# Layer 2's linear attention: the output projection in three products of rounded parts, squares summed on ScalarE, shared buffers

## The chip, the cores and the metric

The kernel runs on one core of a Trainium2 chip. The metric is the device time of one execution in microseconds; the time before is the median of three runs. A core has five engines that run their own queues of instructions in order and wait for one another by semaphores: TensorE (matrix products, "PE"; its weight loads are "PEld"), VectorE ("DVE"), ScalarE ("ACT"), GpSimd ("POOL") and SyncE ("SP"), which issues DMA transfers. Products go into PSUM, everything else lies in SBUF, 128 partitions each.

## What is computed

The reference is a model of four layers over 4 x 512 tokens of 256 channels in fp32; each layer adds an attention part and a feed-forward part to its input. The change is in the attention part of layer 2, a linear attention with 16 heads of 64 key, 64 slot and 128 value channels:

```python
q, k, v = heads(x @ Wq), heads(x @ Wk), heads(x @ Wv)
s = clip(heads(x @ Ws), -32, 32)
# per head, over time t, with p, g from the running log-sum-exp of s:
hk = hk * g_t + k_t[..., None] * p_t          # then ok_t = q_t . hk
pv = softmax(ok)
hv = hv * g_t[..., None] + p_t[..., None] * v_t   # then ov_t = pv_t . hv
g = x @ Wg
o = o * rsqrt(mean(o * o) + EPS) * g_norm_weight
o = o * (g * sigmoid(g))
y = o.reshape(b, t, VALUE_DIM) @ Wo
```

## The kernel before

The layers run one after the other, in blocks that each end at a barrier. The block of the change is `layer2_abc` (L987). Its work is cut into 32 units: 8 pairs of heads times 4 sequences of 512 tokens; `k` is a unit's place in a round of 8, `u` its number. Each engine has a function `unit` that is called 32 times, and its text is the order of the work: nothing is reordered by a scheduler. The projections of unit u + 1 are computed inside unit u, and the output of unit u - 1 is finished there.

TensorE in a unit (L1283 on): the scores of keys and queries (`scores`), the sums of each chunk of 128 tokens (`chunk_sums`), the projections s, k and q of the next unit, the logits (`ok`), the turn of the last unit's output (`turn_out`), v0, the turn of the logits, v1, the **output projection** of the last unit (`emit`, L1209), g0, the turn of the softmax weights, g1, `weights`, the turns of k and e, and `ov`, the output proper. The input projections are products of rounded parts: `split_matmul` (L108) multiplies hi by hi, hi by lo and lo by hi, where hi is the value rounded to a shorter format (fp32r) and lo what is left. The output projection (L1215) is a plain fp32 product of `w_o` and `oT`, which the trace shows as two records each.

Between a unit's output and its projection lies a chain over four engines. `pov`, in the PSUM tensor `pde`, holds the output. ScalarE squares it into `sq`, which is the buffer `on` (L1376). VectorE sums the squares of each head and chunk and scales the sum (`mean_square`, L1460 and 1461). GpSimd raises it to the power -1/2 (`rstd`, L1112) and multiplies the gate with it (`gr`, L1116). VectorE multiplies output and gate (`gated`, L1466), TensorE turns the product into `pde` (L1206), ScalarE multiplies with the norm's weight (`oT`, L1356), and TensorE projects. VectorE adds the result to `x` (L1472).

The head-pair weights are loaded by SyncE into `w_raw`, two slots, and split into `w_hi` and `w_lo` by ScalarE (L1326) and GpSimd (L1098) once for four units; the first slot is split by ScalarE and VectorE at the end of the block before (L401, L393). The weights of the output projection went unsplit into `w_o` with the same call of `load`.

Of the kernel before, what the change touches and what calls it, by code (L numbers as in the profile page):

```python
# [952 lines left out]
class AbcWeights:  # L953


    WQ, WC = 3 * DC * P, 3 * DC * P + 2 * DC * 2 * P

    def __init__(self, st, dram, raw):
        self.dram, self.PV = dram, 2 * P
        self.raw, self.parts = raw, st.sb_parts("w", [P, 2, self.WC])  # L960
        self.o = st.sb("w_o", [P, 2, 2, D])
        self.arrived, self.hi_ready, self.split = [st.sem("w0_in"), st.sem("w1_in")], st.sem("w_hi"), st.sem("w_split")
# [4 lines left out]
    def vg(self, t, slot):  # L967
        return t[:, slot, self.WQ:self.WC].rearrange("p (k c n) -> p k c n", k=2, c=DC)

    def load(self, sp, slot, hp):  # L970
        for k, n in enumerate(("Ws", "Wq", "Wk")):
            sp.dma_start(self.qks(self.raw, slot)[:, k, :, :],
                         in_chunks(self.dram["L2_attn_" + n])[:, :, bass.ds(hp * P, P)]
                         ).then_inc(self.arrived[slot], 16)
        for k, n in enumerate(("Wv", "Wg")):
            sp.dma_start(self.vg(self.raw, slot)[:, k, :, :],
                         in_chunks(self.dram["L2_attn_" + n])[:, :, bass.ds(hp * self.PV, self.PV)]
                         ).then_inc(self.arrived[slot], 16)
        sp.dma_start(self.o[:, slot, :, :], in_chunks(self.dram["L2_attn_Wo"])[:, bass.ds(hp * 2, 2), :]
                     ).then_inc(self.arrived[slot], 16)  # L980
# [6 lines left out]
def layer2_abc(nc, st, core, dram, a, w, aT, w2):  # L987
# [22 lines left out]
    w_raw, w_in_parts, w_o, w_qks, w_vg, load = w.raw, w.parts, w.o, w.qks, w.vg, w.load  # L1010
    gnorm = st.sb("gnorm", [P, 1])
    qT, kT, eT = (st.sb(n, [P, 2, T]) for n in ("qT", "kT", "eT"))
    rT, lgT = st.sb("rT", [P, 2, T]), st.sb("lgT", [P, T])
    k_tok, e_tok = (st.sb(n, [P, 2, NCH, P]) for n in ("k_tok", "e_tok"))
    v, gate = (st.sb(n, [P, 2, NCH, PV]) for n in ("v", "gate"))
    th = st.sb("th", [P, NCH, PV])
    sm, am = st.sb("sm", [P, 2, NCH, P]), st.sb("am", [P, 2, NCH, P])
    hk, hv = st.sb("hk", [P, 3, DK]), st.sb("hv", [P, 3, DV])
    lg, ex, wt = (st.sb(n, [P, NCH, P]) for n in ("lg", "ex", "wt"))
    wT = st.sb("wT", [P, T])  # L1020
    mx, den = st.sb("mx", [P, 8]), st.sb("den", [P, 8])
    on, gr = (st.sb(n, [P, 2, NCH, DV]) for n in ("on", "gr"))
    sq = on
    ms, rstd = st.sb("ms", [P, 8]), st.sb("rstd", [P, 8])
    oT = st.sb("oT", [P, 2, T])
# [9 lines left out]
             "gr_ready on_ready o_turned oT_ready y_ready y_added").split()  # L1035
# [28 lines left out]
    heads8 = lambda a: a.rearrange("t c (h m) -> t (c h) m", h=2)  # L1064

# [12 lines left out]
    with nc.Block() as block:  # L1078
# [15 lines left out]
        def _(pool):  # L1094
# [6 lines left out]
            def unit(u, k, first, last):  # L1101
# [3 lines left out]
                if u and split_in(0, (u - 1) % PER) and not ((u - 1) % PER == 5 and last_round(u - 1)):  # L1105
# [5 lines left out]
                pool.wait_ge(s["ms_step"], 2 * (u + 1))  # L1111
                pool.tensor_tensor(rstd[:], ms[:], core.consts[:, C_HALF:C_HALF + 8], ALU.pow  # L1112
# [3 lines left out]
                pool.tensor_tensor(gr[:].rearrange("t h c v -> t c h v"),  # L1116
                                   gate[:, k % 2].rearrange("t c (h v) -> t c h v", h=2),
# [7 lines left out]
        def _(pe):  # L1125
# [83 lines left out]
            def emit(u, k):  # L1209
                slot = (k // B) % 2  # L1210
                pe.wait_ge(s["oT_ready"], u + 1)
                for t in range(NCH):
                    for h in range(2):
                        cols = oT[:, h, :].rearrange("d (g q p) -> d g p q", q=P, p=2)[:, t // 2, t % 2, :]
                        ins = pe.matmul(pyy[:, t, :], cols, w_o[:, slot, h, :], start=(h == 0), stop=(h == 1))  # L1215
                ins.then_inc(s["y_ready"], 1)
# [103 lines left out]
        def _(act):  # L1320
# [22 lines left out]
            def project_g(u, k, half):  # L1343

                act.wait_ge(s["g_ready"], 2 * u + half + 1)
                act.activation(th[:, 2 * half:2 * half + 2], bank(f"g{half}")[:].rearrange("t (c v) -> t c v", v=PV),  # L1346
                               ACT.Tanh, scale=0.5).then_inc(s["tanh_ready"], 1)
# [6 lines left out]
            def emit(u):  # L1354
                act.wait_ge(s["o_turned"], u + 1)
                act.activation(oT[:], pde[:], ACT.Copy, scale=gnorm[:, 0:1]).then_inc(s["oT_ready"], 1)  # L1356

            def unit(u, k, first, last):
# [17 lines left out]
                act.activation(sq[:], pov, ACT.Square).then_inc(s["sq_ready"], 1)  # L1376
# [20 lines left out]
        def _(dve):  # L1397
# [22 lines left out]
            def project_g(u, k, half):  # L1420
                c = slice(2 * half, 2 * half + 2)
                dve.wait_ge(s["tanh_ready"], 2 * u + half + 1)
                dve.scalar_tensor_tensor(out=gate[:, k % 2, c], in0=th[:, c], scalar=1.0,
# [32 lines left out]
            def mean_square(u):  # L1456

                dve.wait_ge(s["sq_ready"], u + 1)
                do = Steps(dve, s["ms_step"], 2 * u, 2)
                do(dve.reduce_sum(ms[:], sq[:].rearrange("t h c v -> t (h c) v"), AX.X))  # L1460
                do(dve.tensor_scalar(ms[:], ms[:], 4.0 / DV, 4e-5, ALU.mult, ALU.add))  # L1461
                do.close()

            def gated(u):
                dve.wait_ge(s["gr_ready"], u + 1)
                dve.tensor_tensor(on[:], pov, gr[:], ALU.mult).then_inc(s["on_ready"], 1)  # L1466
# [7 lines left out]
            def unit(u, k, first, last):  # L1474
# [17 lines left out]
                if not last:  # L1492
                    project_r(n, kn, 0)
                dve.wait_ge(s["lg_turned"], u + 1)
# [12 lines left out]
                if not last:  # L1507
                    project_r(n, kn, 1)
# [4 lines left out]
                if not last:  # L1513
                    project_g(n, kn, 0)
                    project_g(n, kn, 1)
                mask("am_sums", am, "am_ready", u)
# [13 lines left out]
            gated(HP * B - 1)  # L1530
            rn.part_rows(dve, 1)
# [2074 lines left out]
```

## Time and profile before

| | |
|---|---|
| median of 3 runs | 2144.66 us (2143.91 to 2145.52) |
| the profiled execution's own time | 2147.38 us |
| its span | 2145.6 us |
| TensorE busy over the span | 1849.3 us, 86% |
| VectorE busy | 1379.3 us, 64% |
| ScalarE busy | 676.3 us, 32% |
| GpSimd busy | 572.1 us, 27% |
| mean granted clock of TensorE | 0.925 of full speed |

The profile comes from one execution. Durations overlap within an engine: an instruction can start before the record of the one ahead has ended. Shares over the span are means over stages with different limits, and the stage of the change covers about 530 to 1329 us of it. A row gives the line of the kernel's text, the engine, the operation, and the tensors as out<-in; "a_" stands ahead of the names of this stage. In the brackets behind a row stands how long its engine had been idle and which instruction released it.

### The profile page before, as it was taken

The numbers are of one execution on the slowest core, as the hardware profiler recorded it, in microseconds if no ns is written. First come the engines' busy times: TensorE is split into PE (matmuls) and PEld (weight loads), VectorE is DVE, ScalarE is ACT, GpSimd is POOL, SyncE is SP. The second block draws the span as 40 slices with busy tenths as digits, with TensorE's granted clock in tenths as the row PEclk, the third lists the DMA queues.
The fourth block names the chain that finished last, engine by engine and source line by source line (L and its number), as shares of the span: only waits on it lengthen the run. The fifth ranks groups of instructions, "written<-read, shape, count | busy, mean of one in ns | idle before, by whom it ended". The sixth has DMA issues, their size and how long they took to land. (4 is left out here: it accounts for less than half of the span.)

```text
span 2145.6 us, 35729 instructions
## 1 busy us (share of the span) xinstructions
PE 1849.3 (86%) x13482; PEld 1430.4 (67%) x13482; DVE 1379.3 (64%) x2933; ACT 676.3 (32%) x1202; POOL 572.1 (27%) x550
## 2 busy tenths in 40 slices
PE   5954369963999999999999996999988987989995
PEld 2342257741889998899989994455567876756663
DVE  4478445538778777877777775666656777533334
ACT  2223324431333232333323232135534323222221
POOL 0234725550021221212121212622232104401111
PEclk9976779985999999999999998989998996999998
DMA  8419334435000000000000100000001006111114
GB/s 311 143 51 296 117 113 154 145 116 163 1 1 23 3 22 23 1 23 1 23 1 23 33 1 1 1 1 2 2 1 52 28 4 243 70 38 45 48 47 135
DMA packets 102863, 134.58 MB, mean 63 GB/s; under 512 B 11568, under 2 KB 78796, under 8 KB 102192
## 3 DMA queue, kind: packets, MB, share of 16 engines
q1 hardware_dynamic: 91616, 101.89, 15.1%
q0 software_dynamic: 11088, 30.49, 4.0%
q8 instruction: 109, 1.79, 0.4%
q14 instruction: 50, 0.41, 0.1%
HBM read 81.80 MB, written 50.54 MB: 62 GB/s over the span
## 5 line engine op out<-in xcount | busy, mean ns | idle before, releaser
L1112 POOL TENSOR_TENSOR a_rstd<-a_ms,consts 128x8 f32<-128x8 f32 x32 | 52.3, 1636 | 584.0 <-DVE a_ms L1461 584.0
L110 PE MATMUL a_ring<-a_w_hi,l_xnT_hi 128*128 128x256 f32 x512 | 157.5, 308 | 0.0
L110 PE MATMUL a_ring<-a_w_hi,l_xnT_lo 128*128 128x256 f32 x512 | 144.4, 282 | 0.0
L110 PE MATMUL a_ring<-a_w_lo,l_xnT_hi 128*128 128x256 f32 x512 | 144.1, 282 | 0.0
L2447 POOL DMA_INDIRECT l_slots_in<-xn,f_row_of x96 | 103.9, 1082 | 83.5 <-DVE f_row_of L2757 36.7
L2990 POOL DMA_INDIRECT l_pairs_out<-f_yb,f_to_row x96 | 97.3, 1013 | 94.9 <-ACT f_yb L2965 67.6
L1215 PE MATMUL a_pab<-a_w_o,a_oT 128*128 128x256 f32 x512 | 120.5, 390 | 1.2 <-ACT a_oT L1356 1.2
L1418 DVE RECIPROCAL a_rT<-a_rT 128x256 f32<-128x256 f32 x64 | 111.5, 1744 | 0.0
L1215 PEld LDWEIGHTS a_pab<-a_w_o,a_oT 128*128 128x128 f32 x512 | 101.2, 203 | 11.9 <-ACT a_oT L1356 1.6
L1699 PE MATMUL b_ring<-b_keys,b_qm 32*128 32x128 f32 (+2 forms) x896 | 94.2, 347 | 14.9 <-DVE b_nm L1912 9.4
L1865 ACT ACTIVATE b_work<-b_ring 128x1024 f32<-128x1024 f32 (+1 forms) x96 | 81.1, 881 | 65.1 <-PE b_ring L1706 64.2
L1460 DVE TENSOR_REDUCE a_ms<-a_on 128x8 f32<-128x1024 f32 x32 | 39.1, 1220 | 97.1 <-ACT a_on L1376 97.1
L2884 PE MATMUL f_pgu<-f_gate_up_w,f_xT 128*128 x384 | 94.3, 389 | 6.2 <-ACT f_xT L2945 6.2
L110 PEld LDWEIGHTS a_ring<-a_w_lo,l_xnT_hi 128*128 128x128 f32 x512 | 97.4, 190 | 0.8
L1699 PEld LDWEIGHTS b_ring<-b_keys,b_qm 32*128 32x128 f32 x896 | 67.1, 198 | 46.2 <-issue 23.2
L110 PEld LDWEIGHTS a_ring<-a_w_hi,l_xnT_hi 128*128 128x128 f32 x512 | 97.2, 190 | 0.8 <-issue 0.2
L110 PEld LDWEIGHTS a_ring<-a_w_hi,l_xnT_lo 128*128 128x128 f32 x512 | 97.0, 189 | 0.0
L3096 POOL DMA_INDIRECT l_pairs_out<-f_yb,f_to_row x39 | 37.4, 959 | 211.4 <-ACT f_yb L3178 211.4
L319 PE MATMUL n_turned<-consts,xn 128*128 128x128 f32 x96 | 25.9, 406 | 78.6 <-DVE xn L288 78.6
L3015 DVE TENSOR_TENSOR f_gu<-f_pgu,f_bias 128x256 f32<-128x256 f32 x96 | 40.8, 425 | 74.5 <-issue 40.4
L1706 PE MATMUL b_ring<-b_qm,b_keys 32*128 32x384 f32 (+3 forms) x512 | 87.4, 463 | 0.0
L1346 ACT ACTIVATE a_th<-a_ring 128x512 f32<-128x512 f32 x64 | 38.2, 597 | 154.7 <-PE a_ring L110 154.7
(494 smaller groups left out, 5009.5 us busy)
## 6 DMA issues: line engine op xcount, KB each, us to landing
l_slots_in<-l_zeros SPq DMA_DIRECT2D x4, 3120.0 KB, 22.3
f_xb<-l_slots_in SPq DMA_DIRECT2D x11, 1040.0 KB, 5.9
f_gate_up_w<-l_pairs_out SPq DMA_DIRECT2D x16, 512.0 KB, 8.7
l_slots_in<-l_zeros SPq DMA_DIRECT2D x3, 1690.0 KB, 18.6
f_xb<-l_slots_in SPq DMA_DIRECT2D x39, 130.0 KB, 2.1
f_down_w<-L_ffn_w_down_dram SPq DMA_DIRECT2D x1, 4096.0 KB
f_gate_w<-L_ffn_w_dram SPq DMA_DIRECT2D x2, 2048.0 KB, 10.3
f_up_w<-L_ffn_w_dram SPq DMA_DIRECT2D x2, 2048.0 KB, 18.7
```

Source lines behind the costliest of these rows:

```text
L110: ins = pe.matmul(out, a, b, start=start and k == 0, stop=stop and k == 2, **kw)
L1112: pool.tensor_tensor(rstd[:], ms[:], core.consts[:, C_HALF:C_HALF + 8], ALU.pow).then_inc(s["rstd_ready"], 1)
L1215: ins = pe.matmul(pyy[:, t, :], cols, w_o[:, slot, h, :], start=(h == 0), stop=(h == 1))
L1418: dve.reciprocal(rT[:, k % 2, cols], rT[:, k % 2, cols]).then_inc(s["r_ready"], 1)
L1460: do(dve.reduce_sum(ms[:], sq[:].rearrange("t h c v -> t (h c) v"), AX.X))
L1699: return pe.matmul(ps[:, i, at:at + k1 - k0], qm[strip(j), p, c, b * T + q * P:b * T + (q + 1) * P], keys[strip(j), p, c, b * T + k0:b * T ...
L1706: return pe.matmul(ps[:, i, at:at + T - kb * P], keys[strip(j), p, c, b * T + kb * P:b * T + (kb + 1) * P], qm[strip(j), p, c, b * T + kb ...
L1865: act.activation(probs[:, g % 2, 2 * pair:2 * pair + 2, T_AT[k]:T_AT[k] + w], slot["t", g, pair, k][:, :, 0:w], ACT.Exp).then_inc(s["exp_r ...
L2447: pool.indirect_dma_start(self.xs[:, :], bass.IndirectOffsetOnAxis(ap=self.row_of[:, k, t:t + 1], axis=0), core.rows[:, t, :], None).then_ ...
L2884: ins = pe.matmul(pgu[:, i % 2, j * 2 * I:(j + 1) * 2 * I], xT[:, i % 2, (j * DC + c) * P:(j * DC + c + 1) * P], r.gate_up[:, bass.ds(e, 1 ...
L2990: pool.indirect_dma_start(r.ys[:, :], bass.IndirectOffsetOnAxis(ap=r.to_row[:, b:b + 1], axis=0), yb[:, i % YR, j, :], None).then_inc(stor ...
L3015: dve.tensor_tensor(gu[:, i % GR, j].rearrange("p k i -> p (k i)"), pgu[:, i % 2, j * 2 * I:(j + 1) * 2 * I], r.bias[:, bass.ds(e, 1), :, ...
```

## The change

The output weights are loaded into `w_raw` behind the others and split with them, so that the split covers 2304 instead of 1792 columns. The output projection uses `split_matmul`: 24 products of rounded parts in place of 8 of fp32. For that `oT` becomes two tensors: ScalarE writes the rounded half `oT.hi`, and VectorE writes the rest `oT.lo` in a new step, `split_out`. The projection waits for both. ScalarE's square becomes eight squares, one for each head and chunk, each with its sum taken in the same instruction (`accum_out`), and VectorE's reduction goes away; the scaled sum has a tensor of its own, `msq`. `th` and `gr` go away, their values are kept in `gate`; `lg` and `ex` share `wt`, and `lgT` shares `wT`. VectorE does three steps in another place. Repeated context is cut:

```diff
@@ -953,19 +953,22 @@
...
-    WQ, WC = 3 * DC * P, 3 * DC * P + 2 * DC * 2 * P
+    WQ, WV = 3 * DC * P, 3 * DC * P + 2 * DC * 2 * P
+    WC = WV + 2 * D
...
-        self.o = st.sb("w_o", [P, 2, 2, D])
...
-        return t[:, slot, self.WQ:self.WC].rearrange("p (k c n) -> p k c n", k=2, c=DC)
+        return t[:, slot, self.WQ:self.WV].rearrange("p (k c n) -> p k c n", k=2, c=DC)
+
+    def out(self, t, slot):
+        return t[:, slot, self.WV:self.WC].rearrange("p (h n) -> p h n", h=2)
...
@@ -976,7 +979,7 @@
...
-        sp.dma_start(self.o[:, slot, :, :], in_chunks(self.dram["L2_attn_Wo"])[:, bass.ds(hp * 2, 2), :]
+        sp.dma_start(self.out(self.raw, slot), in_chunks(self.dram["L2_attn_Wo"])[:, bass.ds(hp * 2, 2), :]
...
@@ -1007,22 +1010,23 @@
...
-    w_raw, w_in_parts, w_o, w_qks, w_vg, load = w.raw, w.parts, w.o, w.qks, w.vg, w.load
+    w_raw, w_in_parts, w_out, w_qks, w_vg, load = w.raw, w.parts, w.out, w.qks, w.vg, w.load
...
-    rT, lgT = st.sb("rT", [P, 2, T]), st.sb("lgT", [P, T])
+    rT = st.sb("rT", [P, 2, T])
...
-    th = st.sb("th", [P, NCH, PV])
...
-    lg, ex, wt = (st.sb(n, [P, NCH, P]) for n in ("lg", "ex", "wt"))
+    wt = st.sb("wt", [P, NCH, P])
+    lg = ex = wt
...
+    lgT = wT
...
-    on, gr = (st.sb(n, [P, 2, NCH, DV]) for n in ("on", "gr"))
+    on = st.sb("on", [P, 2, NCH, DV])
...
-    ms, rstd = st.sb("ms", [P, 8]), st.sb("rstd", [P, 8])
-    oT = st.sb("oT", [P, 2, T])
+    ms, msq, rstd = (st.sb(n, [P, 8]) for n in ("ms", "msq", "rstd"))
+    oT = st.sb_parts("oT", [P, 2, T])
...
@@ -1062,6 +1066,9 @@
...
+
+    def gated_by(k):
+        return gate[:, k % 2].rearrange("t c (h v) -> t c h v", h=2)
...
@@ -1108,13 +1115,12 @@
...
-                pool.wait_ge(s["ms_step"], 2 * (u + 1))
-                pool.tensor_tensor(rstd[:], ms[:], core.consts[:, C_HALF:C_HALF + 8], ALU.pow
+                pool.wait_ge(s["ms_step"], u + 1)
+                pool.tensor_tensor(rstd[:], msq[:], core.consts[:, C_HALF:C_HALF + 8], ALU.pow
...
-                pool.tensor_tensor(gr[:].rearrange("t h c v -> t c h v"),
-                                   gate[:, k % 2].rearrange("t c (h v) -> t c h v", h=2),
+                pool.tensor_tensor(gated_by(k), gated_by(k),
...
@@ -1209,10 +1215,13 @@
...
+                pe.wait_ge(s["oT_split"], u + 1)
...
-                        cols = oT[:, h, :].rearrange("d (g q p) -> d g p q", q=P, p=2)[:, t // 2, t % 2, :]
-                        ins = pe.matmul(pyy[:, t, :], cols, w_o[:, slot, h, :], start=(h == 0), stop=(h == 1))
+                        ins = split_matmul(
+                            pe, pyy[:, t, :],
+                            oT.view(lambda x: x[:, h, :].rearrange("d (g q p) -> d g p q", q=P, p=2)[:, t // 2, t % 2, :]),
+                            w_in_parts.view(lambda x: w_out(x, slot)[:, h, :]), start=(h == 0), stop=(h == 1))
...
@@ -1343,7 +1352,7 @@
...
-                act.activation(th[:, 2 * half:2 * half + 2], bank(f"g{half}")[:].rearrange("t (c v) -> t c v", v=PV),
+                act.activation(gate[:, k % 2, 2 * half:2 * half + 2], bank(f"g{half}")[:].rearrange("t (c v) -> t c v", v=PV),
...
@@ -1353,7 +1362,7 @@
...
-                act.activation(oT[:], pde[:], ACT.Copy, scale=gnorm[:, 0:1]).then_inc(s["oT_ready"], 1)
+                act.activation(oT.hi[:], pde[:], ACT.Copy, scale=gnorm[:, 0:1]).then_inc(s["oT_ready"], 1)
...
@@ -1373,7 +1382,11 @@
...
-                act.activation(sq[:], pov, ACT.Square).then_inc(s["sq_ready"], 1)
+                for h in range(2):
+                    for c in range(NCH):
+                        i = h * NCH + c
+                        act.activation(sq[:, h, c, :], pov[:, h, c, :], ACT.Square, accum_out=ms[:, i:i + 1]
+                                       ).then_inc(s["sq_ready"], 1)
...
@@ -1420,7 +1433,7 @@
...
-                dve.scalar_tensor_tensor(out=gate[:, k % 2, c], in0=th[:, c], scalar=1.0,
+                dve.scalar_tensor_tensor(out=gate[:, k % 2, c], in0=gate[:, k % 2, c], scalar=1.0,
...
@@ -1455,15 +1468,20 @@
...
-                dve.wait_ge(s["sq_ready"], u + 1)
-                do = Steps(dve, s["ms_step"], 2 * u, 2)
-                do(dve.reduce_sum(ms[:], sq[:].rearrange("t h c v -> t (h c) v"), AX.X))
-                do(dve.tensor_scalar(ms[:], ms[:], 4.0 / DV, 4e-5, ALU.mult, ALU.add))
-                do.close()
+                dve.wait_ge(s["sq_ready"], 8 * (u + 1))
+                if u:
+                    dve.wait_ge(s["rstd_ready"], u)
+                dve.tensor_scalar(msq[:], ms[:], 4.0 / DV, 4e-5, ALU.mult, ALU.add).then_inc(s["ms_step"], 1)
...
-                dve.tensor_tensor(on[:], pov, gr[:], ALU.mult).then_inc(s["on_ready"], 1)
+                dve.tensor_tensor(on[:], pov, gated_by(u).rearrange("t c h v -> t h c v"), ALU.mult
+                                  ).then_inc(s["on_ready"], 1)
+
+            def split_out(u):
+                dve.wait_ge(s["oT_ready"], u + 1)
+                dve.scalar_tensor_tensor(out=oT.lo[:], in0=pde[:], scalar=gnorm[:, 0:1], in1=oT.hi[:].bitcast(F32),
+                                         op0=ALU.mult, op1=ALU.subtract).then_inc(s["oT_split"], 1)
...
@@ -1491,6 +1509,8 @@
...
+                if not first:
+                    split_out(u - 1)
...
@@ -1504,16 +1524,16 @@
...
-                if not last:
-                    project_r(n, kn, 1)
...
+                    project_r(n, kn, 1)
+                mask("am_sums", am, "am_ready", u)
+                if not last:
...
-                mask("am_sums", am, "am_ready", u)
...
@@ -1528,6 +1548,7 @@
...
+            split_out(HP * B - 1)
```

VectorE, in the middle of a unit, from the product with the gate (`a_on`) to the maximum of the logits (`a_mx`). Before:

```order
L1466 TENSOR_TENSOR a_on<-a_pde,a_gr 128x1024
L1407 COPY a_kT<-a_ring 128x512
L1412 SCALAR_TENSOR_TENSOR a_rT<-consts,a_eT 128x512
L1491 TENSOR_TENSOR a_lgT<-a_pc,a_rT 128x512
L1418 RECIPROCAL a_rT<-a_rT 128x256
L1496 TENSOR_REDUCE a_mx<-a_pc 128x8
L1497 TENSOR_TENSOR a_lg<-a_pc,a_mx 128x512
L1502 TENSOR_REDUCE a_den<-a_ex 128x8
```

Now:

```order
L1478 TENSOR_TENSOR a_on<-a_pde,a_gate 128x1024
L1420 COPY a_kT<-a_ring 128x512
L1425 SCALAR_TENSOR_TENSOR a_rT<-consts,a_eT 128x512
L1509 TENSOR_TENSOR a_wT<-a_pc,a_rT 128x512
L1431 RECIPROCAL a_rT<-a_rT 128x256
L1483 SCALAR_TENSOR_TENSOR a_oT_lo<-a_pde,a_gnorm,a_oT_hi 128x1024
L1516 TENSOR_REDUCE a_mx<-a_pc 128x8
L1517 TENSOR_TENSOR a_wt<-a_pc,a_mx 128x512
L1522 TENSOR_REDUCE a_den<-a_wt 128x8
```

The subtraction `a_oT_lo` stands between the first half of the reciprocal (`a_rT`) and the maximum; the product with the gate reads `a_gate`.

VectorE, in the last third of the unit, from the softmax's division (`a_wt`) to the next unit's first mask (`a_sm`). Before:

```order
L1503 RECIPROCAL a_den<-a_den 128x8
L1505 TENSOR_TENSOR a_wt<-a_ex,a_den 128x512
L1418 RECIPROCAL a_rT<-a_rT 128x256
L1472 TENSOR_TENSOR x<-a_pab,x 128x1024
L1512 TENSOR_TENSOR a_wT<-a_pc,a_rT 128x512
L1423 SCALAR_TENSOR_TENSOR a_gate<-a_th,a_ring 128x512 x2
L1430 TENSOR_TENSOR a_am<-a_pab,consts 128x512 x2
L1460 TENSOR_REDUCE a_ms<-a_on 128x8
L1461 TENSOR_SCALAR a_ms<-a_ms 128x8
L1430 TENSOR_TENSOR a_sm<-a_pab,consts 128x512 x2
```

Now:

```order
L1517 TENSOR_TENSOR a_wt<-a_pc,a_mx 128x512
L1522 TENSOR_REDUCE a_den<-a_wt 128x8
L1523 RECIPROCAL a_den<-a_den 128x8
L1525 TENSOR_TENSOR a_wt<-a_wt,a_den 128x512
L1490 TENSOR_TENSOR x<-a_pab,x 128x1024
L1530 TENSOR_TENSOR a_wT<-a_pc,a_rT 128x512
L1436 SCALAR_TENSOR_TENSOR a_gate<-a_gate,a_ring 128x512
L1431 RECIPROCAL a_rT<-a_rT 128x256
L1443 TENSOR_TENSOR a_am<-a_pab,consts 128x512 x2
L1436 SCALAR_TENSOR_TENSOR a_gate<-a_gate,a_ring 128x512
L1474 TENSOR_SCALAR a_msq<-a_ms 128x8
L1443 TENSOR_TENSOR a_sm<-a_pab,consts 128x512 x2
```

The second half of the reciprocal moved behind the first half of the gate, the second half of the gate behind the two masks (`a_am`), and the reduction into `a_ms` is gone.

ScalarE, at the end of a unit, from the gate's tanh to the next unit's exponential. Before:

```order
L1346 ACTIVATE a_th<-a_ring 128x512 x2
L1330 ACTIVATE a_k_tok<-a_ring 128x512
L1330 ACTIVATE a_e_tok<-a_ring 128x512
L1376 ACTIVATE a_on<-a_pde 128x1024
L1337 ACTIVATE a_eT<-a_eT 128x512
L1330 ACTIVATE a_qT<-a_ring 128x512
```

Now:

```order
L1355 ACTIVATE a_gate<-a_ring 128x512 x2
L1339 ACTIVATE a_k_tok<-a_ring 128x512
L1339 ACTIVATE a_e_tok<-a_ring 128x512
L1388 ACTIVATE a_on,a_ms<-a_pde 128x128 x8
L1346 ACTIVATE a_eT<-a_eT 128x512
L1339 ACTIVATE a_qT<-a_ring 128x512
```

One square became eight of 128 columns that also write `a_ms`; nothing else moved on this engine.

## Rows read from the trace of the kernel before

**Rows 1.** The windows view of eight units: length, PE, PEld, DVE, ACT, POOL busy, clock, DMA
```profile
829.10:1021.40 192.30, 192.30 (x1748) 173.47 (x1746) 150.03 (x224) 61.15 (x90) 36.53 (x18) 1.00 0.04 13
```

**Rows 2.** The timeline of TensorE in one unit: scores, projection, turn, next scores
```profile
1021.39 1.16 PE L1177 MATMUL a_pab<-a_qT,a_kT 64*128 64x128 f32 x16
...
1033.89 3.34 PEld L1215 LDWEIGHTS a_pab<-a_w_o,a_oT 128*128 128x128 f32 x16
...
1037.47 0.19 PEld L110 LDWEIGHTS a_ring<-a_w_lo,l_xnT_hi 128*128 128x128 f32 x1
...
1038.79 0.47 PEld L1242 LDWEIGHTS a_pc<-consts,a_wt 128*128 128x128 f32 x4
...
1045.42 1.16 PE L1177 MATMUL a_pab<-a_qT,a_kT 64*128 64x128 f32 x16
```

**Rows 3.** The timeline of ScalarE and GpSimd in the same unit
```profile
1021.50 1.02 ACT L1376 ACTIVATE a_on<-a_pde 128x1024 f32<-128x1024 f32 x1 [1.14 <-PE a_pde L1268]
...
1030.91 1.12 ACT L1356 ACTIVATE a_oT<-a_pde,a_gnorm 128x1024 f32<-128x1024 f32 x1 [2.10 <-PE a_pde L1206]
...
1024.06 1.64 POOL L1112 TENSOR_TENSOR a_rstd<-a_ms,consts 128x8 f32<-128x8 f32 x1 [20.40 <-DVE a_ms L1461]
1025.77 1.92 POOL L1116 TENSOR_TENSOR a_gr<-a_gate,a_rstd 128x1024 f32<-128x1024 f32 x1
```

**Rows 4.** The timeline of VectorE in the same unit
```profile
1022.55 1.22 DVE L1460 TENSOR_REDUCE a_ms<-a_on 128x8 f32<-128x1024 f32 x1 [3.11 <-ACT a_on L1376]
...
1027.72 1.23 DVE L1466 TENSOR_TENSOR a_on<-a_pde,a_gr 128x1024 f32<-128x1024 f32 x1
...
1032.84 0.64 DVE L1496 TENSOR_REDUCE a_mx<-a_pc 128x8 f32<-128x512 f32 x1
...
1035.92 0.69 DVE L1505 TENSOR_TENSOR a_wt<-a_ex,a_den 128x512 f32<-128x512 f32 x1
...
1042.18 1.28 DVE L1430 TENSOR_TENSOR a_am<-a_pab,consts 128x512 f32<-128x512 f32 x2
```

**Rows 5.** The timeline of TensorE in layer 2's experts: 12 three-part products of 256 columns
```profile
1650.85 0.28 PE L110 MATMUL f_py<-f_w_hi,f_hidden_hi 128*128 128x256 f32 x1
...
1652.28 0.39 PE L110 MATMUL f_pg<-f_a_hi,f_w_hi 128*128 128x512 f32 x1
```

**Rows 6.** The timeline of ScalarE: accumulator reads in layer 3, plain copies in layer 1
```profile
1825.44 0.19 ACT L3379 ACTIVATION_READ_ACCUMULATOR a_pr<-a_ps,a_nmax 128x1 f32 x1
1825.60 0.37 ACT L3379 ACTIVATE a_pr<-a_pw,a_nmax 128x128 f32<-128x128 f32 x1
1825.86 0.19 ACT L3379 ACTIVATION_READ_ACCUMULATOR a_pr<-a_pw,a_nmax 128x1 f32 x1
...
229.34 0.38 ACT L897 ACTIVATE a_sums<-a_out 128x256 f32<-128x256 f32 x1 [0.82 <-PE a_out L849]
229.62 0.30 ACT L885 ACTIVATE a_vals<-xn 128x128 f32 x1
```

**Rows 7.** The lines view, shapes apart: count, busy us, mean ns of one
```profile
L2381 DVE SCALAR_TENSOR_TENSOR x<-f_py,f_cw,x 128x256 f32<-128x256 f32 x128 | 52.8, 475 | 0.3 <-PE f_py L110 0.3
...
L2372 DVE TENSOR_TENSOR f_hidden_lo<-f_raw,f_hidden_hi 128x512 fp32r<-128x512 f32 x32 | 26.6, 832 | 0.0
...
L389 DVE TENSOR_TENSOR l_xnT_lo<-n_turned,l_xnT_hi 128x256 fp32r<-128x256 f32 x16 | 6.6, 422 | 0.9 <-ACT l_xnT_hi L403 0.9
```

**Rows 8.** The timeline of a wait of TensorE for VectorE in the stage's first unit
```profile
557.32 0.69 DVE L1505 TENSOR_TENSOR a_wt<-a_ex,a_den 128x512 f32<-128x512 f32 x1
...
558.07 0.42 PEld L1242 LDWEIGHTS a_pc<-consts,a_wt 128*128 128x128 f32 x4 [1.49 <-DVE a_wt L1505]
```

**Rows 9.** The timeline ahead of the stage's first unit, and behind its last
```profile
521.31 1.69 ACT L401 ACTIVATE a_w_hi<-a_w_raw 128x1792 fp32r<-128x1792 f32 x1
...
527.58 2.02 DVE L393 TENSOR_TENSOR a_w_lo<-a_w_raw,a_w_hi 128x1792 fp32r<-128x1792 f32 x1
...
1322.52 6.08 PE L1215 MATMUL a_pab<-a_w_o,a_oT 128*128 128x256 f32 x16 [1.20 <-ACT a_oT L1356]
```

More of the change, by code:

```diff
@@ L1034, in layer2_abc @@
              "den_step wt_ready w_turned wT_ready am_sums am_ready ov_ready sq_ready ms_step rstd_ready "
-             "gr_ready on_ready o_turned oT_ready y_ready y_added").split()
+             "gr_ready on_ready o_turned oT_ready oT_split y_ready y_added").split()
     s = {n: sem(n) for n in names}
```

## The prediction

> **What bounds the kernel now.** I read the page first. The chain that ended last is followed back only into layer 3, so it says nothing of the stage that changes, and the busy shares are means over all stages. So I went to layer 2's linear attention, from about 530 to 1329 us, whose 32 units repeat one pattern of instructions. The windows view of eight units [rows 1] shows TensorE busy for the whole stretch at full clock (2.4 GHz), VectorE for 78% of it, ScalarE for a third, GpSimd for a fifth. The timeline of TensorE [rows 2] gives the period: scores begin at 1021.39 and again at 1045.42, 24.03 us per unit. TensorE is the bound here, which makes its time the first thing to look at, and the waits of the other engines harmless as long as they stay covered.
>
> The second thing is how much cover they have. Behind the scores' start one chain runs over four engines [rows 3, 4]: ScalarE squares the last unit's output 0.11 us later for 1.02, VectorE reduces for 1.22 and scales, GpSimd raises to the power (1.64) and multiplies the gate (1.92, ending 1027.69), VectorE multiplies the output at 1027.72, and then works without a gap through kT, the scan, lgT and half of the reciprocal until the maximum starts at 1032.84. TensorE's output projection, which needs the product turned and scaled by ScalarE (ready at 1032.03), starts its loads at 1033.89. Until now 1.9 us lie between the two.
>
> **What the change takes from TensorE.** Eight fp32 products of 256 columns, 16 records, become 24 products of rounded parts. Before, the first load starts at 1033.89 and the second load of the group behind it at 1037.47 [rows 2]: 3.58 us with one product of 0.12 in it. The nearest row for the new form is exact: the down projection of layer 2's experts multiplies the same strided columns, rounded, in three parts with 256 columns, and 12 of them take 1652.28 - 1650.85 = 1.43 us [rows 5], 0.119 each. 25 of them are 2.98, so TensorE's work shrinks by 0.60 us per unit. If nothing waited, 30 units would give 18 us.
>
> Here a rule of the Trainium skill says more: its page "FP8 and Floating Point Precision" (TensorE Precision Notes) gives true fp32 as four passes through the array. Three passes for four would take a quarter of the 3.46 us of the old group, 0.87 us and not 0.60. The rows don't give that much, since a short product has a cost beside its columns; the rule's result is a rival below.
>
> **What it puts into the chain: squares.** ScalarE now makes eight squares of 128 columns, each with a sum in its accumulator, where there was one square of 1024 and a reduction on VectorE. The stage has no such instruction; layer 3's softmax has [rows 6]. There each ACTIVATE with accumulator is followed by an own ACTIVATION_READ_ACCUMULATOR of 0.193 us; the next ACTIVATE starts 0.16 behind the read's start (1825.44 to 1825.60), the read 0.10 ahead of the ACTIVATE's end. That ACTIVATE has a bias by pointer and takes 0.37; a square without one, by the step from 1024 columns (1.02) to 256 (0.38) [rows 3, 6], some 0.275 for 128. Then a read would start 0.175 after its square, and a pair costs 0.175 + 0.16 = 0.335. Bounds: 0.27, if the next square may overlap a read by the 0.10 by which plain copies overlap (229.34 to 229.62 for one of 0.38), and 0.43, the pair with a pointer as it stands. I take 0.335, because the 0.16 is seen directly. Eight pairs end at 1021.50 + 7 x 0.335 + 0.175 + 0.193 = 1024.21. The reduction that they replace ended at 1023.77 [rows 4]. So the scaling, the power, the gate and the product with it come 0.44 us later, one for one, since VectorE already waits for the gate there (1027.69 to 1027.72). The bounds give -0.01 and +1.2.
>
> The Trainium skill's page "ScalarE: Activation LUTs" (What ACT_TABLE_LOAD costs) gives an ACTIVATE with immediates 186 ns and 0.833 per column, consecutive ones overlapping by 93, and knows no separate read. By it eight squares would take 8 x 0.2 = 1.6 us, and the chain would get earlier. The trace shows the read in rows 6; whether it comes for squares too no row of before shows, hence the second rival.
>
> **What it puts into the chain: the low part.** VectorE must now subtract the rounded output from the unrounded (oT_lo), 1024 columns from PSUM, put between the reciprocal's first half and the maximum. These are the places in the order shown for VectorE. Nearest rows: a product of 1024 columns with PSUM takes 1.23 [rows 4]; a scalar by pointer adds 0.05 (475 against 422 ns) [rows 7]; so 1.28. Bounds: 1.23, and 1.66, twice the 832 ns of rows 7 for 512 rounded columns, which is a subtraction of two operands in SBUF; this one reads PSUM as the 422 ns row does, so I stay by 1.28. It starts at 1032.84 + 0.44 = 1033.28, ends at 1034.55, and TensorE follows 0.06 later (557.32 + 0.69 = 558.01 to 558.07) [rows 8]: 1034.61 in place of 1033.89, 0.72 later. Behind a wait, loads and products close up by 0.05 (four turns take 0.42 and not 0.47) [rows 2, 8], which leaves 0.67. ScalarE's rounded half is ready by about 1032.3 and isn't what is waited for. With TensorE's 0.60 returned, a unit is **0.07 us longer**, 30 units 2.0 us (bounds of the pair: -0.38 and +0.8 each; of the subtraction: 0 and +0.45).
>
> That is the whole point of this forecast: the 0.60 us that TensorE no longer works it waits, because the projection is now released by VectorE: even without the slip of the squares the subtraction would end at 1034.12, past the 1033.89 of before.
>
> **What I cost at nothing.** The maximum starts 1.63 later, so the softmax weights are done at 1038.24 (1035.92 + 0.69 + 1.63) [rows 4]; TensorE wants them at 1038.79 + 0.07 [rows 2]: covered by 0.6, and were this gone, each tenth would count. VectorE's total does not change (reduction 1.22 out, subtraction 1.28 in). The second half of the reciprocal moves behind the first half of the gate and the second gate half behind the masks; the masks began at 1042.18 and move by less than half a microsecond, which TensorE's product with them has to give, barely. The sums for the state come up to 0.44 later, so the q projection may wait a few tenths, but TensorE is then still ahead of 1034.6. Splitting weights grows by 512 of 1792 columns: ScalarE and GpSimd do this seven times while otherwise idle. The buffers that are shared are each read for the last time long before the next write; the gate in place is the same 1024 columns for GpSimd. The DMA for the output weights goes to another place with the same bytes, on the same queue in the same order.
>
> **Ends of the stage.** The first split lies on the path [rows 9]: ScalarE's 1.69 grows by 0.43, VectorE's 2.02, the last thing ahead of the stage, by 0.53; together 1.0. Behind the last unit nothing is hidden: the squares cost 0.44 more, the subtraction and its wait 1.33, the last unit itself some 0.2, and the projection, 6.08 with the clock partly at its lower level [rows 9], saves some 0.55: 1.4. Sum: 2.0 + 1.0 + 1.4 = **4.4 us** on the profiled execution's 2147.38, which is 2151.8; the median of the runs shown is 2.72 below it, so 2149.1. I give 2149. A difference of 0.2% (4.3 us) is about what can be told from none, so this lies on the border between the two verdicts.
>
> **Rivals.** *Cheap reads.* The next square overlaps the read, a pair is 0.27: the slip is gone, the projection's load waits until 1034.17, and a unit gains 0.38: -12 + 2 on 2147.4, less the 2.7: 2135. For it: plain ACTIVATEs overlap by 0.10; against it: the 0.16 of rows 6. With no reads at all TensorE waits for nothing, 30 x 0.60 less 1 for the ends: 2128. *A dear subtraction.* It writes rounded numbers at the 832 ns per 512 of rows 7: 0.38 more in every unit, 30 times, and at the end: 2161. It decides as soon as it takes over 1.3 us. For it: that row writes the same type; against: the 422 ns row does too. *Pairs of 0.43.* Slip 1.2, +0.8 per unit: 2173. For it: the only pair in the trace; against: its pointer. *Three for four passes.* The new group is 3 quarters of the old 3.46, 2.60: 0.27 more gained per unit, 2141 (the Trainium skill's rule above); against it rows 5. *The change does nothing to the path*, VectorE being hidden: excluded, since TensorE's wait for the low part is in every unit, unless the squares get cheap.
>
> **Chances.** My forecast with 2145 to 2153 around it 0.53, cut in two by the border; cheap reads 0.14, none 0.06; dear subtraction 0.11; pairs of 0.43 0.06; the three-for-four rule 0.05; other things 0.05. Faster by over 0.2%: 0.14 + 0.06 + 0.04 of the rest, 0.24. Within 0.2%: 0.27 + 0.05, 0.32. Slower: 0.26 + 0.11 + 0.06 + 0.01, 0.44. The range from 2134 to 2161 takes in cheap reads and the dear subtraction and leaves out the two outermost.
>
> **What would show it.** In the profile after: a READ_ACCUMULATOR behind each square and pairs of 0.33 (a last read that ends 2.8 us after the scores' start); 24 records at 0.119 for the projection; VectorE's a_oT_lo at 1.28; TensorE waiting some tenths in each unit for a_oT_lo; a period of 24.0 to 24.2 us. I am wrong if TensorE stays without waits, if the period falls under 23.8, or if another wait (the turn of the softmax weights, the products with am) stands in the list.

## The result, and the profile after

| | before | changed |
|---|---|---|
| median | 2144.66 us (5 runs, 2143.91 to 2146.43) | 2132.88 us (5 runs, 2132.04 to 2134.97) |
| the profiled execution's own time | 2147.38 us | 2133.99 us |
| its span | 2145.6 us | 2132.2 us |

The changed kernel is 0.5% faster: the ratio is 0.9948, with a 95% interval from 0.9936 to 0.9959, 11.8 us by the medians. The forecast was 2149, so the sign was wrong, and the time lies 1.1 us under the lower end of its range.

TensorE in a unit, as in [rows 2]: products and weight loads from the scores to the next unit's scores.

```profile
1013.68 1.16 PE L1183 MATMUL a_pab<-a_qT,a_kT 64*128 64x128 f32 x16
...
1026.06 0.19 PEld L110 LDWEIGHTS a_ring<-a_w_hi,l_xnT_lo 128*128 128x128 f32 x1
...
1026.33 0.19 PEld L110 LDWEIGHTS a_pab<-a_w_hi,a_oT_hi 128*128 128x128 f32 x1
...
1029.33 0.19 PEld L110 LDWEIGHTS a_ring<-a_w_lo,l_xnT_hi 128*128 128x128 f32 x1
...
1030.66 0.46 PEld L1251 LDWEIGHTS a_pc<-consts,a_wt 128*128 128x128 f32 x4
...
1037.29 1.16 PE L1183 MATMUL a_pab<-a_qT,a_kT 64*128 64x128 f32 x16
```

The period is 1037.29 - 1013.68 = 23.61 us (24.03 before). The projection's first load comes 12.65 us behind the scores' start, where it came 12.50 behind; from it to the second load of the next group pass 3.00 us, where it was 3.58. To the turn of the softmax weights it is 4.33 in place of 4.90. TensorE's group lost 0.57 us, and 0.15 of it came back as a wait ahead of it. The wait can be read from the loads: the projection's first starts 0.27 us behind the load ahead of it (1026.06 to 1026.33), where before it was 0.12 (to 1033.89 [rows 2]), the usual distance:

```profile
1033.77 0.19 PEld L110 LDWEIGHTS a_ring<-a_w_hi,l_xnT_lo 128*128 128x128 f32 x1
```

ScalarE in the same unit: the first two squares and the last, each with its read (start, duration).

```profile
1013.79 0.28 ACT L1388 ACTIVATE a_on<-a_pde 128x128 f32<-128x128 f32 x1 [1.14 <-PE a_pde L1277]
1013.96 0.19 ACT L1388 ACTIVATION_READ_ACCUMULATOR a_on<-a_pde 128x1 f32 x1
1014.05 0.27 ACT L1388 ACTIVATE a_on<-a_pde 128x128 f32<-128x128 f32 x1
1014.21 0.20 ACT L1388 ACTIVATION_READ_ACCUMULATOR a_on<-a_pde 128x1 f32 x1
...
1015.55 0.32 ACT L1388 ACTIVATE a_on<-a_pde 128x128 f32<-128x128 f32 x1
1015.71 0.25 ACT L1388 ACTIVATION_READ_ACCUMULATOR a_on<-a_pde 128x1 f32 x1
```

A pair of a square and its read takes 0.25 us: the read starts 0.16 to 0.17 behind its square, the next square 0.09 behind the read. The last read ends at 1015.96, 2.28 us behind the scores. The reduction that it replaces ended 2.38 us behind them [rows 4].

GpSimd and VectorE, which take the sum up from there, as in [rows 3, 4]:

```profile
1016.25 1.64 POOL L1119 TENSOR_TENSOR a_rstd<-a_msq,consts 128x8 f32<-128x8 f32 x1 [19.97 <-DVE a_msq L1474]
1017.97 1.92 POOL L1123 TENSOR_TENSOR a_gate<-a_gate,a_rstd 128x1024 f32<-128x1024 f32 x1
```

```profile
1016.00 0.17 DVE L1474 TENSOR_SCALAR a_msq<-a_ms 128x8 f32<-128x8 f32 x1 [3.52 <-ACT a_on L1388]
...
1019.92 1.22 DVE L1478 TENSOR_TENSOR a_on<-a_pde,a_gate 128x1024 f32<-128x1024 f32 x1 [0.21 <-POOL a_gate L1123]
...
1025.03 1.18 DVE L1483 SCALAR_TENSOR_TENSOR a_oT_lo<-a_pde,a_gnorm,a_oT_hi 128x1024 fp32r<-128x1024 f32 x1
1026.13 0.68 DVE L1516 TENSOR_REDUCE a_mx<-a_pc 128x8 f32<-128x512 f32 x1
...
1029.27 0.69 DVE L1525 TENSOR_TENSOR a_wt<-a_wt,a_den 128x512 f32<-128x512 f32 x1
...
1034.27 1.22 DVE L1443 TENSOR_TENSOR a_am<-a_pab,consts 128x512 f32<-128x512 f32 x2
```

The product with the gate starts 6.24 us behind the scores and not 6.33. The low part a_oT_lo takes 1.18 us and ends 12.53 behind them, 0.12 ahead of the projection's first load. The division's result is ready at 1029.96, 0.70 ahead of the load of TensorE's turn at 1030.66. The windows view of the changed kernel, the stretch of [rows 1]:

```profile
829.10:1021.40 192.30, 192.30 (x1837) 174.72 (x1837) 150.96 (x231) 73.27 (x212) 40.62 (x19) 1.00 0.05 14
```

TensorE is counted as busy for the whole stretch, in this kernel too, although it waits 0.15 us in every unit. The ends of products in the profile are modelled, and the wait lies within the record of the product ahead of it; the distance of starts shows it, the busy time and the list of waits don't.

The ends of the stage, as in [rows 9], with the stage's first product (L110):

```profile
520.90 2.11 ACT L401 ACTIVATE a_w_hi<-a_w_raw 128x2304 fp32r<-128x2304 f32 x1
...
527.58 2.55 DVE L393 TENSOR_TENSOR a_w_lo<-a_w_raw,a_w_hi 128x2304 fp32r<-128x2304 f32 x1
...
530.45 0.77 PE L110 MATMUL a_ring<-l_xnT_hi,a_w_hi 128*128 128x512 f32 x1 [3.67 <-PEq L416]
...
1310.52 0.55 PE L110 MATMUL a_pab<-a_w_hi,a_oT_hi 128*128 128x256 f32 x1 [2.62 <-DVE a_oT_lo L1483]
...
1315.11 0.82 PE L319 MATMUL a_ring<-consts,a_v 128*128 128x128 f32 x6
```

The stage's first product before:

```profile
529.92 0.76 PE L110 MATMUL a_ring<-l_xnT_hi,a_w_hi 128*128 128x512 f32 x1 [3.14 <-PEq L416]
```

From the start of ScalarE's split to this product it was 8.61 us (521.31 to 529.92) and is 9.55 (520.90 to 530.45), 0.94 more. The first unit's scores come only 0.55 us later (543.96 for 543.41), because the blocks ahead, which do the same in both kernels, happened to bring the split 0.41 earlier in this execution. From the last unit's scores to the next block's first product it takes 46.77 us, 0.94 less than before (1273.32 to 1320.09, and 1285.68 to 1333.39). The 31 distances from unit to unit give 12.9 (742.27 from the first unit's scores to the last's, now 729.36). Together 12.9 + 0.9 - 0.55 = 13.3 us of the 13.4 by which the span is shorter.

### The profile page after: what moved, and what is told of

Same layout as the page of the kernel before. It is cut to its first block and busy times, and to the rows that moved or that the text cites. A ratio compares the mean times of both kernels' runs of the same rounds, so it can differ in the third digit from the quotient of the medians.

```text
span 2132.2 us, 36753 instructions
## 1 busy us (share of the span) xinstructions
PE 1836.1 (86%) x13738; PEld 1425.0 (67%) x13738; DVE 1370.9 (64%) x2933; ACT 719.6 (34%) x1682; POOL 577.1 (27%) x550
## 5 line engine op out<-in xcount | busy, mean ns | idle before, releaser
L1119 POOL TENSOR_TENSOR a_rstd<-a_msq,consts 128x8 f32<-128x8 f32 x32 | 52.4, 1637 | 555.8 <-DVE a_msq L1474 555.8
L110 PE MATMUL a_ring<-a_w_hi,l_xnT_hi 128*128 128x256 f32 x512 | 152.0, 297 | 0.0
L110 PE MATMUL a_ring<-a_w_hi,l_xnT_lo 128*128 128x256 f32 x512 | 144.5, 282 | 0.0
L110 PE MATMUL a_ring<-a_w_lo,l_xnT_hi 128*128 128x256 f32 x512 | 144.3, 282 | 0.0
L1720 PE MATMUL b_ring<-b_keys,b_qm 32*128 32x128 f32 (+2 forms) x896 | 94.2, 347 | 14.9 <-DVE b_nm L1933 9.4
L110 PEld LDWEIGHTS a_ring<-a_w_lo,l_xnT_hi 128*128 128x128 f32 x512 | 97.6, 191 | 0.0
L110 PEld LDWEIGHTS a_ring<-a_w_hi,l_xnT_hi 128*128 128x128 f32 x512 | 97.5, 190 | 0.2 <-issue 0.2
L110 PEld LDWEIGHTS a_ring<-a_w_hi,l_xnT_lo 128*128 128x128 f32 x512 | 97.4, 190 | 0.0
L319 PE MATMUL n_turned<-consts,xn 128*128 128x128 f32 x96 | 26.1, 412 | 80.6 <-DVE xn L288 80.6
L1852 POOL TENSOR_SCALAR_AFFINE_SELECT b_work<-b_work 128x256 f32<-128x256 f32 x128 | 50.5, 407 | 127.2 <-ACT b_work L1886 125.2
L3227 DVE COPY f_hT<-f_ph 128x512 f32<-128x512 f32 x39 | 27.0, 691 | 87.8 <-PE f_ph L3157 87.8
L110 PE MATMUL a_ring<-l_xnT_hi,a_w_hi 128*128 128x512 f32 x192 | 79.7, 415 | 3.7 <-PEq L416 3.7
L2905 PEld LDWEIGHTS f_pgu<-f_gate_up_w,f_xT 128*128 128x128 f32 x384 | 70.5, 194 | 17.3 <-issue 9.0
## 6 DMA issues: line engine op xcount, KB each, us to landing
f_up_w<-L_ffn_w_dram SPq DMA_DIRECT2D x2, 2048.0 KB, 19.1
```

What stands on the lines that cost most here:

```text
L110: ins = pe.matmul(out, a, b, start=start and k == 0, stop=stop and k == 2, **kw)
L1119: pool.tensor_tensor(rstd[:], msq[:], core.consts[:, C_HALF:C_HALF + 8], ALU.pow).then_inc(s["rstd_ready"], 1)
L1720: return pe.matmul(ps[:, i, at:at + k1 - k0], qm[strip(j), p, c, b * T + q * P:b * T + (q + 1) * P], keys[strip(j), p, c, b * T + k0:b * T ...
L2905: ins = pe.matmul(pgu[:, i % 2, j * 2 * I:(j + 1) * 2 * I], xT[:, i % 2, (j * DC + c) * P:(j * DC + c + 1) * P], r.gate_up[:, bass.ds(e, 1 ...
```

## The experiments

All eight kernels start from the changed one, each timed against the kernel before. They were run in two groups on two chips (before: 2144.1 for the first four, 2144.4 for the last four), so across the groups the ratios and the periods are to be compared. The edits are shown shortened; `...` stands for what is left out. A period is the distance from one unit's scores to the next's. Theory: the gain is TensorE's shorter group less the wait for the low part, and the forecast failed at the spacing of the squares. Its main rivals: the gain is VectorE's (its reduction went), or that of the squares and the order.

**proj_only**: one square and VectorE's reduction as before.

```diff
-                for h in range(2):
-                    for c in range(NCH):
...
-                        act.activation(sq[:, h, c, :], pov[:, h, c, :], ACT.Square, accum_out=ms[:, i:i + 1]
...
+                act.activation(sq[:], pov, ACT.Square).then_inc(s["sq_ready"], 1)
...
+                do(dve.reduce_sum(ms[:], sq[:].rearrange("t h c v -> t (h c) v"), AX.X))
...
```

> The changed kernel with one square of 1024 columns and VectorE's reduction as before; the projection in three products, the buffers and VectorE's order stay changed. Theory (the whole gain is TensorE's shorter group, 0.57 us in each of 30 units, less 0.15 us of waiting for the low part): the chain up to the product with the gate is 0.09 us longer (6.33 against 6.24 us behind the scores' start), the projection starts that much later, 30 x 0.09 = 2.8 us more than the changed kernel: 2135.7. Rival (VectorE's lost reduction is what brings the gain): near the kernel before, 2144.

Measured 2136.72 (2134.50 to 2138.23), ratio to before 0.9964 (0.9950 to 0.9977). Its scores, timeline of TensorE:

```profile
1014.78 1.16 PE L1183 MATMUL a_pab<-a_qT,a_kT 64*128 64x128 f32 x16
...
1038.47 1.16 PE L1183 MATMUL a_pab<-a_qT,a_kT 64*128 64x128 f32 x16
```

A period of 23.69, 0.08 above the changed kernel. The new projection without the squares brings 7.4 us, most of the gain; the squares add the 0.1 us by which they end earlier in each unit.

**squares_only**: the projection in fp32 again, no low part, weights of the projection unsplit.

```diff
-                pe.wait_ge(s["oT_split"], u + 1)
...
-                        ins = split_matmul(
...
+                        ins = pe.matmul(pyy[:, t, :], cols, w_o[:, slot, h, :], start=(h == 0), stop=(h == 1))
...
-                dve.scalar_tensor_tensor(out=oT.lo[:], in0=pde[:], scalar=gnorm[:, 0:1], in1=oT.hi[:].bitcast(F32),
...
```

> The changed kernel with the projection undone: eight fp32 products, an unsplit weight tensor, no low part and no subtraction; the eight squares with sums, the shared buffers and VectorE's order stay changed. Theory: TensorE is without gaps as before and has the same work, so 2144.7, no difference. Rival (the squares and the order bring the gain): 2136 or less.

Measured 2143.89 (2142.81 to 2147.17), ratio 0.9998 (0.9989 to 1.0007). TensorE's scores again 24.02 apart:

```profile
1021.16 1.16 PE L1184 MATMUL a_pab<-a_qT,a_kT 64*128 64x128 f32 x16
...
1045.18 1.16 PE L1184 MATMUL a_pab<-a_qT,a_kT 64*128 64x128 f32 x16
```

Squares, shared buffers and VectorE's new order are together worth nothing while the projection is fp32. The theory holds; the two rivals, VectorE's lost reduction and the squares with the order, fall.

**late_wait**: TensorE waits for the low part ahead of the first product that reads it.

```diff
-                pe.wait_ge(s["oT_split"], u + 1)
                 for t in range(NCH):
                     for h in range(2):
-                        ins = split_matmul(
...
+                        pe.matmul(pyy[:, t, :], left.hi, right.hi, start=(h == 0), stop=False)
+                        pe.matmul(pyy[:, t, :], left.hi, right.lo, start=False, stop=False)
+                        if t == 0 and h == 0:
+                            pe.wait_ge(s["oT_split"], u + 1)
+                        ins = pe.matmul(pyy[:, t, :], left.lo, right.hi, start=False, stop=(h == 1))
```

> The changed kernel, in which TensorE waits for the low part only ahead of the third product, the first that reads it, instead of ahead of the first. Theory: the wait of 0.15 us in each unit is shorter than two products of 0.12 and goes: 30 x 0.15 = 4.4 us less, 2128.4, a period of 23.46 us. Rival (the next wait, for the turned softmax weights or the products with am, takes its place, or TensorE was never waiting there): 2132.9.

Measured 2125.17 (2120.30 to 2126.77, 4 runs), ratio 0.9904 (0.9889 to 0.9920).

```profile
1010.44 1.16 PE L1183 MATMUL a_pab<-a_qT,a_kT 64*128 64x128 f32 x16
...
1033.91 1.16 PE L1183 MATMUL a_pab<-a_qT,a_kT 64*128 64x128 f32 x16
```

The period is 23.47, as expected. From the first unit's scores to the last's it takes 725.25 us against 729.36: 4.1 less. The span is 8.2 less. Of the rest 3.1 us lie in the block behind the stage (see the last section), 0.3 behind the last unit, and 0.6 ahead of the first unit, where both kernels do the same.

**ptr_scale**: the squares take their scale, 1.0, by pointer.

```diff
-ACT.Square, accum_out=ms[:, i:i + 1]
+ACT.Square, scale=core.consts[:, C_ONE:C_ONE + 1], accum_out=ms[:, i:i + 1]
```

> The changed kernel, in which each of the eight squares takes its scale (1.0) by pointer. It measures why the forecast's pair of 0.335 us was 0.25. Theory A (a read holds up the next ACTIVATE only where that has a pointer operand, as in layer 3: 0.26 to the read and 0.16 behind it, 0.42 a pair): the chain slips by 8 x 0.17 = 1.4 us in each unit, TensorE already waits for it, so 30 x 1.4 = 41 us more, 2174. Theory B (the pointer adds its 0.09 to the ACTIVATE alone): a pair of 0.34, 0.75 a unit, 22 us more, 2155. Theory C (it is neither, layer 3's spacing has another cause): near 2133.

Measured 2156.01 (2155.10 to 2157.36), ratio 1.0056 (1.0042 to 1.0070). ScalarE, and TensorE's scores:

```profile
1026.60 0.37 ACT L1388 ACTIVATE a_on<-a_pde,consts 128x128 f32<-128x128 f32 x1 [1.14 <-PE a_pde L1277]
1026.87 0.19 ACT L1388 ACTIVATION_READ_ACCUMULATOR a_on<-a_pde,consts 128x1 f32 x1
1026.96 0.36 ACT L1388 ACTIVATE a_on<-a_pde,consts 128x128 f32<-128x128 f32 x1
1027.21 0.20 ACT L1388 ACTIVATION_READ_ACCUMULATOR a_on<-a_pde,consts 128x1 f32 x1
```

```profile
1002.17 1.16 PE L1183 MATMUL a_pab<-a_qT,a_kT 64*128 64x128 f32 x16
...
1026.49 1.16 PE L1183 MATMUL a_pab<-a_qT,a_kT 64*128 64x128 f32 x16
```

Theory B: the ACTIVATE is 0.09 longer, the next one still starts 0.09 behind the read, a pair is 0.34 and the period 24.32. Eight pairs of 0.09 are 0.72, and 0.71 arrive at TensorE: with the wait in place the chain from the squares to the projection is passed on one for one. This kernel is slower than before, with the same work on TensorE as the changed one. So the 0.16 between a read and the next ACTIVATE in layer 3 needs another cause, and the trace of before has it, with VectorE's and ScalarE's rows side by side:

```profile
1825.27 0.29 DVE L3408 TENSOR_REDUCE a_nmax<-a_pw 128x1 f32<-128x128 f32 x1
...
1872.54 0.29 DVE L3408 TENSOR_REDUCE a_nmax<-a_pw 128x1 f32<-128x128 f32 x1
...
1872.70 0.19 ACT L3379 ACTIVATION_READ_ACCUMULATOR a_pr<-a_ps,a_nmax 128x1 f32 x1
1872.86 0.37 ACT L3379 ACTIVATE a_pr<-a_pw,a_nmax 128x128 f32<-128x128 f32 x1
```

In layer 3 each ACTIVATE waits, by the kernel's text, for the maximum that it takes as bias. The maxima end at 1825.27 + 0.29 = 1825.56 and at 1872.83, and the ACTIVATEs start 0.04 and 0.03 later, at 1825.60 [rows 6] and 1872.86. The last 0.07 of the 0.16 are thus a wait for VectorE. Nothing names it in brackets, because the record of the read, 0.19 us long, covers it.

**old_order**: VectorE's order of before in the last third of the unit.

```diff
+if not last: project_r(n, kn, 1)
 if not first: emit(u - 1, (k - 1) % PER)
...
 project_g(n, kn, 0)
-project_r(n, kn, 1)
+project_g(n, kn, 1)
 mask("am_sums", am, "am_ready", u)
-project_g(n, kn, 1)
```

> The changed kernel with VectorE's order of before in the last third of the unit: the second half of the reciprocal ahead of the addition to x, the second half of the gate ahead of the masks. Theory (the softmax weights now come 1.65 us later in the unit than before, so what stands between them and the product for TensorE's next step is on the path): the reciprocal's 1.66 us puts the end of wT at 33.36 on the trace of the changed kernel, where TensorE's next loads began at 32.71: 0.7 us in each unit, 21 us, 2154. Rival (the order was hidden in both, as it was before the change): 2133.

Measured 2149.25 (2143.98 to 2152.07), ratio 1.0021 (1.0012 to 1.0030).

```profile
1015.73 0.69 DVE L1525 TENSOR_TENSOR a_wt<-a_wt,a_den 128x512 f32<-128x512 f32 x1
1016.34 1.74 DVE L1431 RECIPROCAL a_rT<-a_rT 128x256 f32<-128x256 f32 x1
1018.00 1.16 DVE L1490 TENSOR_TENSOR x<-a_pab,x 128x1024 f32<-128x1024 f32 x1
1019.08 0.68 DVE L1532 TENSOR_TENSOR a_wT<-a_pc,a_rT 128x512 f32<-128x512 f32 x1
...
1019.81 1.16 PE L1262 MATMUL a_pab<-a_wT,a_eT 64*128 64x128 f32 x16 [0.56 <-DVE a_wT L1532]
```

The reciprocal stands between the division and the addition, wT ends at 1019.76, and TensorE starts 0.05 later after a wait that the trace marks (0.56 us). The period is 24.23, 0.62 over the changed kernel, a little less than expected. The expectation put the softmax weights 1.65 us later in the unit than before; on the changed kernel they come 1.06 later (16.28 us behind the scores for 15.22 [rows 4]). So the new order, worth nothing beside the fp32 projection, is worth 16 us beside the new one by the medians (19.1 us in the units of the two traces, 748.42 for 729.36).

**r0_later**: the first half of the reciprocal goes into VectorE's wait for the exponential, behind the subtraction.

```diff
-if not last: project_r(n, kn, 0)
 if not first: split_out(u - 1)
...
 do.close()
+if not last: project_r(n, kn, 0)
 dve.wait_ge(s["ex_ready"], u + 1)
```

> The changed kernel with the first half of the reciprocal moved from ahead of the subtraction to behind the subtraction of the maximum, where VectorE waits 0.77 us for ScalarE's exponential. Theory (TensorE's wait of 0.15 us for the low part is made by VectorE's order alone): the low part is ready 0.7 us earlier, the wait goes, the softmax weights come at about the same time, 30 x 0.15 = 4.4 us less, 2128.4; up to 3 less or more by the clock's state behind the stage. Rival: 2133, the wait moves to another place.

Measured 2127.98 (2127.54 to 2131.35), ratio 0.9929 (0.9915 to 0.9943). VectorE:

```profile
1000.79 1.28 DVE L1483 SCALAR_TENSOR_TENSOR a_oT_lo<-a_pde,a_gnorm,a_oT_hi 128x1024 fp32r<-128x1024 f32 x1 [0.90 <-ACT a_oT_hi L1365]
```

VectorE now idles 0.90 us for ScalarE's half and still has the low part 11.94 us behind the scores (990.13), 0.6 before TensorE comes; the period is 23.47.

**r0_late**: both edits.

> r0_later and late_wait together. Theory: each alone takes the whole wait away and TensorE is then without gaps, so both together give nothing beyond late_wait: a period of 23.46 us, 2125 to 2128. Rival (there is a second hidden wait of VectorE's in each unit): 2 us or more below late_wait.

Measured 2128.15 (2123.63 to 2129.13), ratio 0.9920 (0.9906 to 0.9934); period 23.46. Nothing beyond either alone: there is no second hidden wait that this removes.

**proj_late**: late_wait with one square and the reduction.

> late_wait with one square and VectorE's reduction in place of the eight squares with sums. Theory (the squares are worth 0.09 us of the chain, and only while TensorE waits for the low part): the low part is needed 0.24 us behind the projection's start, 0.24 us is what proj_only waited, so the period is 23.46 to 23.5 and the time that of late_wait within 2 us. Rival (the eight squares matter by themselves): 3 us or more above late_wait.

Measured 2127.17 (2125.64 to 2127.48), ratio 0.9919 (0.9906 to 0.9933); period 23.47. With the wait in the right place the eight squares bring nothing. Four versions are thus faster than the changed kernel: late_wait, r0_later, r0_late and proj_late, at 2125 to 2128 and periods of 23.46 to 23.47; between them the times don't decide.

## Why the prediction was wrong

The forecast said +0.07 us per unit and got -0.42. By its own steps:

- **What TensorE gives back**: 0.60 said, 0.57 measured. The products of rounded parts run at 0.12 us each, as the experts' row had it [rows 5]. The rival "three for four passes" wanted 0.87; the 0.57 decides against it here.
- **The squares, the step that failed**: "a pair costs 0.175 + 0.16 = 0.335", called "seen directly". A pair costs 0.25. The 0.175 was right (0.16 to 0.17); the 0.16 was set by a wait for VectorE and is not the cost of a read, which lets the next square start after 0.09. The slip of +0.44 was -0.09. These 0.53 us account for the 0.49 by which the unit was missed (the small errors below run both ways). On the profiled execution the forecast was 2151.8 and the time 2133.99, 17.8 us less: the units make 14.9 of it, the end behind the last unit 2.3, the start 0.5. The rival "cheap reads" (0.27 a pair, 2135) had the mechanism and almost the size; it got 0.14 of the chance, because one misread row stood against it. The sign of the forecast hung on this one term: with 0.27 a pair the same sum makes the unit 0.38 shorter.
- **The subtraction**: 1.28 said, 1.18 measured in the units; where VectorE has idled ahead of it (r0_later, and behind the last unit) it takes 1.28. The "dear subtraction" falls.
- **The hand-over**: 0.06 less 0.05 for closing up was said; the load started 0.12 behind the subtraction's end and nothing closed up. These errors are small and cancel with the one above (0.11 more, 0.10 less).
- **The wait for the low part is on the path**: right. Taking it away gave 0.13 us per unit, in two different ways, and what was put into the chain arrived (0.71 of 0.72, ptr_scale). With a pair of 0.34, close to the forecast's, the unit is indeed longer than before, 24.32 for 24.03: the mechanism was right and the size of one term wrong. (It is 0.29 and not 0.07, mainly since the last square with its pointer and the last read are longer too.)
- **What was costed at nothing**: right for the shared buffers, the masks and the splitting of weights. The order of VectorE's last third was right too, but I didn't price the move: without it each unit would be 0.62 us longer, more than the 0.42 that the change gains.
- **The ends**: +1.0 said for the start, and it is 0.94 from the split's start on, ScalarE's 0.42 and VectorE's 0.53 both on the path (9.54 to 9.56 us to the first product in the eight kernels with the wider split, 8.60 and 8.61 in the two without). The 0.55 at the first scores holds 0.41 of scatter from the blocks ahead. Behind the last unit -0.94 came for +1.4, in three parts. The last unit, from its scores to the first product of the step behind it (L319), took 23.89 us for 24.84, 0.95 less where 0.2 more was said. From there to the last projection it is 1.31 more (13.31 for 12.00), where the squares and the subtraction were to cost 1.77. The projection took 4.59 us (1310.52 to 1315.11) for 5.91 (1322.52 to 1328.43), 1.32 less and not 0.55: at a granted clock of 0.59 a product of rounded parts mostly takes 0.21 us and not 0.12, so the shorter group saves more.

## What to carry to other kernels

The distance between two instructions of an engine is a cost only if nothing else ends at that moment: ahead of taking a spacing from a row, put the other engines' rows of those microseconds beside it, since a wait that lies within the record of the instruction ahead carries no mark (0.07 us on ScalarE, 0.15 on TensorE here). Where a wait falls among several products, put it ahead of the one that reads the datum. And when work moves from the engine that bounds to one that was hidden, its order there has to be made anew: an order that was worth nothing before can be worth more than the change itself (0.62 us a unit here for 0.42).

## What the runs showed of the hardware

The block behind the stage, up to the experts of layer 2, runs in two lengths. Its first 16.6 us in the changed kernel and in late_wait (windows view, the third value from the end is TensorE's granted clock):

```profile
1320.10:1336.70 16.60, 15.92 (x44) 6.99 (x45) 6.25 (x10) 3.69 (x5) 9.46 (x7) 0.90 0.02 1
```

```profile
1315.10:1331.70 16.60, 15.92 (x48) 7.16 (x49) 7.92 (x12) 4.27 (x6) 10.90 (x8) 1.00 0.02 1
```

In the profiled executions of before, after, squares_only, proj_only and r0_later, where its first four products take 2.8 to 3.3 us, the time from its first product to the experts' first is 290.8 to 291.1 us; in late_wait, proj_late, r0_late, old_order and ptr_scale, where they take 1.95, 287.6 to 288.8. TensorE did the same there in all of them. What differs is the granted clock at its start, 0.90 or 1.00 as a mean of 16.6 us, that is partly at the lower of its two levels (1.2 GHz) or wholly at the upper (2.4 GHz). What sets it I did not settle: in the 23.1 us ahead TensorE is busy for 13.09 us in the changed kernel and for 14.00 in late_wait, at a mean granted clock of 0.70 in both. The two groups lie 2 to 3.5 us apart. About 1.7 of it arise in these first 16.6 us (an estimate: 0.10 of 16.6, and 4 records more); that the rest comes of the clock too isn't shown. It is why late_wait gained 8.2 us of span on 4.1 us of units, and why the four best versions can't be put in order.

An ACTIVATE that sums has a read of 0.19 to 0.25 us by the records, but in a row of squares of 128 columns the next square starts 0.09 us behind the read's start, with a pointer and without (ptr_scale, the changed kernel).
